# A graph network's second message pass: the last seven edge tiles fetched row by row from SyncE

## What is computed

```python
edge_index = jnp.stack([src, dst])
x = x + _L0_gnn_ref(_layernorm(x), edge_index, ...)      # graph attention
x = x + _L0_ffn_ref(_layernorm(x)[None], ...)[0]         # 8 experts, top 2
x = x + _L1_gnn_ref(_layernorm(x), L1_gnn_W, L1_gnn_b, edge_index)
x = x + _L1_ffn_ref(_layernorm(x)[None], ...)[0]         # attention over slices
```

```python
def _L1_gnn_ref(x, W, b, edge_index):
    src, tgt = edge_index[0], edge_index[1]
    xt = jnp.einsum('ni,oi->no', x, W) + b
    out = jax.ops.segment_sum(xt[src], tgt, num_segments=num_nodes)
    deg = jax.ops.segment_sum(jnp.ones_like(tgt, dtype=x.dtype), tgt, num_segments=num_nodes)
    return out / (deg + 1.0)[:, None]
```

## Time and profile before

| | |
|---|---|
| median of 3 runs (lowest, highest) | 1991.83 us (1985.57, 1994.75) |
| profiled execution, its own time | 1993.71 us |
| its span, first to last instruction | 1992.0 us |
| share of the span busy: PE, DVE, ACT, POOL | 68%, 46%, 29%, 55% |
| mean granted TensorE clock | 0.818 |

### The profile page before, as it was taken

One profiled execution on the slowest core, in us unless ns is written; L12 is line 12 of the kernel. 1 busy time (PEld: TensorE's weight loads), 2 busy tenths in 40 slices (PEclk: granted clock), 3 DMA queues, 4 the chain that ended last, 5 costly groups with the idle time before them and its releaser, 6 DMA issues. The chain is left out here.

```text
span 1992.0 us, 23465 instructions
## 1 busy us (share of the span) xinstructions
PE 1356.1 (68%) x6516; PEld 1119.8 (56%) x6516; DVE 908.6 (46%) x1818; ACT 576.6 (29%) x1264; POOL 1103.5 (55%) x1086
## 2 busy tenths in 40 slices
PE   2535666666656266599999997555656657567978
PEld 2324445444444146599999996434444445345757
DVE  7425544444443667533333333643334343337833
ACT  2133433333333014233333332322222222223310
POOL 4477777777773600477222372177777777764510
PEclk7756888777877575699999998888888787878979
DMA  6484998888887602332111023733333333330002
GB/s 143 119 249 150 311 297 284 279 290 282 270 277 239 155 3 73 122 122 81 51 51 51 37 93 81 184 103 106 104 105 105 105 106 104 106 90 1 1 0 65
DMA packets 156807, 268.52 MB, mean 135 GB/s; under 512 B 26747, under 2 KB 119839, under 8 KB 155567
## 3 DMA queue, kind: packets, MB, share of 16 engines
q1 hardware_dynamic: 100252, 135.75, 22.0%
q0 software_dynamic: 46224, 123.97, 20.6%
q10 hardware_dynamic: 10213, 7.36, 1.5%
HBM read 169.82 MB, written 98.15 MB: 135 GB/s over the span
## 5 line engine op out<-in xcount | busy, mean ns | idle before, releaser
L1180 POOL DMA_INDIRECT sum_rows<-xn_tab,src_e x391 | 378.9, 969 | 176.0 <-issue 118.8
L1202 PE MATMUL bank<-sum_held,sum_hot 128*125 128x256 f32 x976 | 301.1, 470 | 205.6 <-ACT sum_held L1212 205.5
L798 POOL DMA_INDIRECT gat_rows<-xh_tab,src_e x363 | 343.6, 946 | 114.8 <-issue 108.4
L1202 PEld LDWEIGHTS bank<-sum_held,sum_hot 128*125 128x125 f32 x976 | 219.6, 233 | 284.0 <-issue 194.4
L871 PE MATMUL bank<-gat_rows,gat_same 128*128 128x264 f32 x784 | 262.2, 481 | 126.0 <-issue 126.0
L871 PEld LDWEIGHTS bank<-gat_rows,gat_same 128*128 128x128 f32 x784 | 175.7, 242 | 165.7 <-issue 132.7
L1212 ACT COPY sum_held<-sum_rows 128x1024 f32 x122 | 127.4, 1045 | 379.2 <-SPq L1171 347.0
L1887 PE MATMUL bank<-weights,e_xthigh 128*128 x896 | 219.8, 329 | 8.6 <-DVE e_xtlow L2042 5.4
L915 ACT COPY gat_outs<-bank 128x528 f32<-128x528 f32 x196 | 117.5, 599 | 285.3 <-PE bank L871 284.9
L1232 DVE SCALAR_TENSOR_TENSOR res<-bank,prep_inv,res 125x256 f32 x122 | 58.9, 483 | 292.1 <-PE bank L1202 288.4
L2047 DVE TENSOR_TENSOR e_h<-e_gated,bank 128x342 f32<-128x342 f32 x112 | 57.1, 510 | 262.5 <-ACT e_gated L1980 262.5
(11 more groups left out here) (506 smaller groups left out, 2418.9 us busy)
## 6 DMA issues: line engine op xcount, KB each, us to landing
parts<-gat_outs SPq DMA_DIRECT2D x27, 1904.0 KB, 8.1
staged<-w_tab SPq DMA_DIRECT2D x8, 2132.0 KB, 8.2
w_tab<-w_stage SPq DMA_DIRECT2D x16, 682.0 KB, 10.7
w_raw<-in_L_ffn_w_dram SPq DMA_DIRECT2D x16, 640.0 KB
gat_rows<-xh_tab,src_e POOLq DMA_INDIRECT x391, 4.4
sum_rows<-xn_tab,src_e POOLq DMA_INDIRECT x391, 2.7
w_tab<-w_stage SPq DMA_DIRECT2D x8, 768.0 KB, 10.6
weights<-y_tab SPq DMA_DIRECT2D x10, 600.0 KB
```

The costliest lines, as they stand in the source:

```text
L798: pool.indirect_dma_start(out=rows[b % R][:, t, :], out_offset=None, in_=k.xh_tab, in_offset=bass.IndirectOffsetOnAxis(ap=k.src_e[:, b * S ...
L1180: pool.indirect_dma_start(out=rows[:, at // IP % (RING * GPAIRS), at % IP, :], out_offset=None, in_=k.xn_tab, in_offset=bass.IndirectOffse ...
L1202: m = nc.tensor.matmul(k.ps[s][0:P, 0:C], hot[g % 2][:, s, c, :], held[:, s, c, :], start=(c == 0), stop=(c == IP - 1))
```

## The change

SyncE fetches the seven used tiles of quads 96 and 97, one edge's vector at a time: 7 x 128 = 896 DMAs of one row. It loads the node's number from `src_e` to a register and issues a DMA from that row of `xn_tab`. The DMAs go to two quads of their own behind the ring, and are spread over the loop: after each quad's `landed` SyncE issues ten of them (`BY_ROW`). GpSimd's loop stops at quad 96 (`LATE`). VectorE's tables send items of the last two quads to slots 16 and 17, and it clears the eighth tile, which has no edges.

```diff
+LATE = GBATCHES - 2
+BY_ROW = 10
...
-        v.tensor_single_scalar(self.slot[:, :], self.pair_i[:, :], RING * GPAIRS - 1, ALU.bitwise_and)
+        me(dve, v.tensor_single_scalar(self.slot[:, :], self.pair_i[:, :], RING * GPAIRS - 1, ALU.bitwise_and))
+        me(dve, v.tensor_copy(self.slot_f[:, :], self.slot[:, :]))
+        me(dve, v.scalar_tensor_tensor(out=self.slot_f[:, :], in0=self.pair[0:1, :], scalar=float(LATE) - 0.5, in1=self.slot_f[:, :], op0=ALU.is_lt, op1=ALU.mult))
+        me(dve, v.tensor_scalar(self.is_late[:, :], self.pair[0:1, :], float(LATE) - 0.5, None, ALU.is_gt))
+        me(dve, v.scalar_tensor_tensor(out=self.is_late[:, :], in0=self.pair[0:1, :], scalar=float(RING - LATE), in1=self.is_late[:, :], op0=ALU.add, op1=ALU.mult))
+        me(dve, v.tensor_tensor(self.slot[:, :], self.slot_f[:, :], self.is_late[:, :], ALU.add))
...
-        rows = sb("rows", [EP, RING * GPAIRS, IP, C])
+        rows = sb("rows", [EP, RING * GPAIRS + GBATCHES - LATE, IP, C])
+        late_in, late_cleared = [sem(f"late_in{a}") for a in range(GBATCHES - LATE)], sem("late_cleared")
+        late_rows = [(p, t) for t in range(USED - LATE * GB) for p in range(EP)]
...
-                sp.wait_ge(rows_in[b % RING], 16 * GB * (b // RING) + 16 * gathered(b, GB))
+                if b < LATE:
+                    sp.wait_ge(rows_in[b % RING], 16 * GB * (b // RING) + 16 * gathered(b, GB))
+                else:
+                    sp.wait_ge(late_cleared, 1)
+                    sp.wait_ge(late_in[b - LATE], 16 * EP * gathered(b, GB))
                 sp.sem_inc(landed, 1)
+                for p, t in late_rows[b * BY_ROW:(b + 1) * BY_ROW]:
+                    node = sp.value_load(k.src_e[p:p + 1, LATE * GB + t:LATE * GB + t + 1], min_val=0, max_val=N - 1)
+                    sp.dma_start(rows[p:p + 1, RING * GPAIRS + t // IP, t % IP, :], k.xn_tab[bass.ds(node, 1), :]).then_inc(late_in[t // IP], 16)
...
-            for b in range(GBATCHES):
+            for b in range(LATE):
...
             v.memset(k.att["square"][:, :, :], 0.0).then_inc(squares0, 1)
+            v.memset(rows[:, RING * GPAIRS + GBATCHES - LATE - 1, IP - 1, :], 0.0).then_inc(late_cleared, 1)
```

More of the change, by code:

```diff
@@ L966, in scratch @@
         self.pick, self.pair_i = sb("pick", [Q, QP, ISLOTS]), sb("pair_i", [1, ISLOTS], I32)
+        self.slot_f, self.is_late = sb("slot_f", [1, ISLOTS]), sb("is_late", [1, ISLOTS])
     def on_pool(self, pool):
@@ L1155, in ring_pair @@
         def ring_pair(eng, n):
-            slot = eng.value_load(w.slot[0:1, n:n + 1], min_val=0, max_val=RING * GPAIRS - 1)
+            slot = eng.value_load(w.slot[0:1, n:n + 1], min_val=0, max_val=RING * GPAIRS + GBATCHES - LATE - 1)
             return rows[:, bass.ds(slot, 1), :, :].rearrange("p a i c -> p (a i c)")
```

## The result

The changed kernel takes 2705.6 us (median of 4 runs, 2704.15 to 2710.71) where the kernel before takes 1988.7 us beside it: a ratio of 1.363, with a 95% interval of 1.360 to 1.366, 717 us more. The profiled execution took 2706.8 us, its span is 2704.6 us.

The account below looks back on a forecast made before the run. GpSimd's gathers were taken to bound the pass; SyncE's row fetches would take over, +501 us to the last signal and +24 us of tail on 1993.7: 2519 us, 2517 against the median, range 2440 to 2820 us.

Parts of the forecast that it names:

- The bound before, and SyncE's room of 4.44 us per quad: Second pass: GpSimd's gathers set the pace, and SyncE can take 4.44 us more per quad before it does.
- SyncE becomes the bound from the first quad on, with GpSimd held back by `room`: Second pass: ten rows per quad exceed SyncE's slack, GpSimd stops for room, signals some 11 us apart, last signal +501 us.
- What a row costs: SyncE's queue: load, register instructions, DMA issue and pauses take 1.04 us per row, 932 us for 896 rows.
- a rival said that each load behind a DMA takes 0.450 us: SyncE's row loads take 0.450 us in place of 0.267: +164 us, 2681 us in all; chance 0.05.
- the likeliest case: Whole kernel: the forecast itself, with issues of 0.24 to about 0.45 us, 2440 to 2670 us; chance 0.70.
- the sum by the row: Whole kernel: SyncE's rows at 1.04 us each plus the tail, 2517 us against the median.
- The tail: End of the pass: some 10 items at 2.8 us remain, 30 us after the last signal instead of 6.4, +24 us.
- The removed gathers, the tables, the clearing: Second pass and VectorE: 8.8 us of gathers saved but worth nothing; tables' some 1.3 us and the clearing covered.
- The rival of slow issues: SyncE's one-row DMAs beside gathers take 0.60 us to issue: +296 us, 2813 us; chance 0.16.
- theory C1: From the experiments: a load is slow because a DMA on one queue leaves SyncE's queue something to finish; otherwise about 0.27 us.

Follow-up runs that it names:

- e11: Changed kernel with only three tiles fetched by row, four rows per quad, GpSimd gathering the other four late tiles: 2053.4 us beside 1990.3, ratio 1.033.
- e10: Changed kernel with only two tiles fetched by row, three rows per quad, GpSimd gathering the other five late tiles: ratio 0.998 to the kernel before.
- e9: Changed kernel with the 896 one-row DMAs from row numbers written in the program, no register loads for them: 1978.7 us beside 1990.3, ratio 0.9955.
- e1: Changed kernel with its tables, extra slots and clearing, but GpSimd gathers all tiles and SyncE fetches no row: 2334.9 us beside 2333.9, ratio 1.0002.
- e3: Changed kernel with the 896 loads but without their DMAs, GpSimd gathering all tiles: 2407 us beside 2334, ratio 1.033.
- e6: Changed kernel with, in each quad, first the ten loads and then the ten DMAs: ratio 1.193 to the kernel before.
- e5: Changed kernel with each row's DMA taking 16 separate pieces of 16 values from two neighbouring rows of another table: ratio 1.324 to the kernel before.

## Why the prediction was right, and where its size was off

*The bound before, and SyncE's room of 4.44 us per quad.* Right. e11, e10 and e9 lie on the expected sides of it.

*SyncE becomes the bound from the first quad on, with GpSimd held back by `room`.* Right: the signals are 12.8 us apart from the first quads on, GpSimd waits 690.8 us for L1179, and SyncE 0.4 us for its own rows. In size they are 12.4 to 13.8 us apart, where some 11 were forecast.

*What a row costs.* Here the size failed. The forecast had 1.04 us, and a row takes 1.242 us in the middle of a quad: 498 + 147 + 18 + 42 + 29 + 255 = 989 ns and pauses of some 250. The pauses were right (0.27 for 0.25), the issue was right (0.27 for 0.255). **The mis-sized term is the load, 0.267 us for 0.498.** Over 896 rows this is 0.231 x 896 = +207 us, less 13 for the issue and 18 for the pauses; the 82 loads of `room` grew from 0.267 to 0.491, +18 us. That makes 194 us by the medians, of the 1195.6 - 988 = 208 us by which the signals took longer than forecast. The first load of a quad was shorter than the median, 9 us in all, and 45 single pauses of over 0.3 us are 15 us.

I had weighed this: a rival said that each load behind a DMA takes 0.450 us, 2681 us in all, and that is the nearest of all the cases. I gave it 0.05, because the one load that the earlier trace rows show behind a DMA took 0.267 us. Its reason was the right one, its figure was luck: the 0.450 us of the earlier trace rows is the first load of `room` alone, 27 us after the last DMA of the queue, and the others took 262 to 277 ns:

```profile
L1168 SPq TENSOR_LOAD <-walk_room x2: 272/361/450, 1324.6 to 1329.6; - x2
L1168 SPq TENSOR_LOAD <-walk_room x80: 262/267/277, 1334.8 to 1732.2; - x80
```

The DMA of the earlier trace rows covers 128 partitions, and the rows' DMAs one. I took its price apart by what it moves when I sized the issue, and forgot to when I sized what comes after it. The result lies within the range, but outside the 2440 to 2670 us that I gave for the likeliest case; the sum by the row, 2517 us, was too low by 189 us.

*The tail.* +24 us were forecast, and it is 18.4 - 6.4 = +12 us. Nine items took 15.78 us, 1.75 us each, where I took 2.8. TensorE was busy nearly all the time in both stretches (15.54 of 16.00 us, and 8.38 of 8.60); the granted clock is what differs. It was 1.00 from 2493 to 2509 us, and 0.64 on the mean in the stretch that I had read (the kernel before; stretch, us, busy us of PE, PEld, DVE, ACT, POOL, granted clock, DMA share, GB/s):

```profile
1768.40:1777.00 8.60, 8.38 (x24) 6.47 (x24) 3.29 (x5) 2.09 (x2) 6.49 (x7) 0.64 0.36 107
```

The ratio of the clocks is 1.56, and that of the times 1.59.

*The removed gathers, the tables, the clearing.* Nothing in the changed kernel, as forecast (e1). VectorE's L1027 of before started at 121.47 us; its counterpart starts at 121.40, with five more operations ahead of it, as the idle time in front of it shrank from 2.81 to 1.17 us. The 8.8 us for seven gathers fit e9, which gained 6 to 12 us.

*The rival of slow issues (0.16)* fell: 255 ns at the median and 299 at most in the changed kernel, and 247 and 372 in e9, beside gathers all the time. What the earlier trace rows show were then not the gathers' doing; whether it was the queue behind the large loads, or the shape, wasn't tried.

What stays open is what makes a load 0.23 us longer right behind the issue of a one-row DMA. e9 shows that the next DMA isn't delayed (0.247 us each), and e3 and e6 that a load is short where no DMA stands right ahead of it (272 ns at the median in both). Issue and load together are nearly constant: 255 + 498 = 753 ns in the changed kernel, 225 + 520 = 745 in e6, 247 + 527 = 774 in e9 (its loads of `room`). So in these kernels a shorter issue just ahead of a load gained little. The loads of rows in e5, 274 ns behind a DMA of 32 packets, fit theory C1, but no run here sees what SyncE's queue would have left to finish, e5 changed the length of the issue too, and its loads of `room` at 702 ns are not explained by it.

## What to carry to other kernels

A queue that waits most of the time has slack, but it is finite and can be read: here it was the 4.44 us of waits per turn of the loop, and three rows a quad fitted (ratio 0.998) while four did not (1.033). Before work moves there, price the whole chain of its instructions with the pauses between them, and take the price from a row with the same neighbours: a load behind a one-row DMA took 498 ns, the load behind a wide one 267. With fetches by register, put the loads together and the DMAs together (1.193 instead of 1.284), load several numbers at once after reading what that load costs (four took 553 ns, three 848 to 926), and stop at what the slack holds.

## What was unexpected of the hardware

What a load on SyncE took differed with what stood before it: 267 ns on its own (`room` in the kernel before), 498 ns right behind a one-row DMA of 2 packets (the changed kernel), 274 ns behind one of 32 (e5), whose issue in turn took 506 instead of 255 ns.

Some loads also took longer when they read another half of the partitions than the load before them. In the changed kernel the first load of a quad follows the load of `room`, from partition 0, with no DMA between. For quads whose first row lies in partitions 0 to 63 it took 269 to 286 ns (40 quads), and in 64 to 127 it took 426 to 442 (42 quads). Right behind a one-row DMA the change of half made no difference (490 and 491 ns for `room`), and behind e5's DMA of 16 pieces it made 707 ns out of 268 (medians). Two loads of the first kind, partition 16 and partition 66:

```profile
L1187 SPq TENSOR_LOAD <-src_e x1: 277/277/277, 1829.4 to 1829.4; - x1
```

```profile
L1187 SPq TENSOR_LOAD <-src_e x1: 426/426/426, 1895.8 to 1895.8; - x1
```

TensorE's clock was lower in the pass of the changed kernel, where it had less work: with a burst of products every 13 us, 34.47 us of 100, the granted clock was 0.59 on the mean from 1800 to 1900 us. The kernel before had 0.83 from 1400 to 1500 us, busy 63.46 us. That the work sets the clock isn't shown: from 1768.4 to 1777 us the kernel before had 0.64 with TensorE busy for 8.38 of 8.60 us. The 976 products took 401.5 us busy instead of 301.1. It cost nothing, since TensorE wasn't the bound. The stretches, the first of the kernel before and two of the changed kernel:

```profile
1400.00:1500.00 100.00, 63.46 (x218) 47.84 (x216) 39.37 (x63) 26.11 (x25) 75.86 (x80) 0.83 0.37 105
```

```profile
1800.00:1900.00 100.00, 34.47 (x87) 25.19 (x88) 15.19 (x23) 10.44 (x10) 29.83 (x32) 0.59 0.14 41
2493.00:2509.00 16.00, 15.54 (x72) 13.12 (x71) 9.71 (x18) 8.16 (x8) 0.00 (x0) 1.00 0.00 1
```
